# Two columns of the horizontal bias in one matmul for two of three thirds, a second copy of the queries, and one buffer for the rounded biases

## What is computed

```python
qkv = (x.reshape(B, S, dim) @ qkv_w + qkv_b).reshape(B, S, 3, nh, hd)
attn = jnp.einsum('bqc,bkc->bqk', q * scale, k)
rel_h = jnp.einsum('bhwc,hkc->bhwk', r_q, Rh)
rel_w = jnp.einsum('bhwc,wkc->bhwk', r_q, Rw)
attn = (attn.reshape(B * nh, h, w, h, w) + rel_h[:, :, :, :, None] + rel_w[:, :, :, None, :]).reshape(B * nh, S, S)
attn = jax.nn.softmax(attn, axis=-1)
out = (attn @ v).reshape(B, nh, h, w, hd)
return out @ proj_w + proj_b
```

## Times and profile before

| | |
|---|---|
| median of 3 runs | 6956.17 us (6955.4 to 11830.54) |
| profiled execution | 6956.88 us, its span 6955.1 us |
| mean granted TensorE clock | 0.988 |
| PE busy | 97% of the span |
| DVE, ACT, POOL busy | 79%, 68%, 13% |
| DMA engines busy | 65%, 146 GB/s on average |

### The profile page before, as it was taken

How to read it: one execution, slowest core, us unless ns; L and a number is a source line. 1 busy time by engine, 2 the same in 40 slices (tenths; PEclk the granted TensorE clock), 3 DMA queues, 4 the chain that set the end, 5 groups by cost and what they waited for, 6 DMA issues and landing times.

```text
span 6955.1 us, 139199 instructions
## 1 busy us (share of the span) xinstructions
PE 6778.3 (97%) x53600; PEld 4259.6 (61%) x53600; DVE 5488.7 (79%) x10165; ACT 4705.9 (68%) x10033; POOL 932.6 (13%) x967
## 2 busy tenths in 40 slices
PE   6999999999999999999999999999999999999998
PEld 4666666666666666666665666656666566666664
DVE  6887888778887788877888778887788878877883
ACT  2777676667666677666776767667676676766775
POOL 2112010110102110121111111102101121101110
PEclk8999999999999999999999999999999999999999
DMA  5667676666767667676666666766667666666663
GB/s 141 143 147 159 135 151 144 157 155 136 152 133 161 148 140 155 141 164 139 148 142 147 156 144 142 154 144 157 143 141 155 137 162 141 141 149 143 147 146 90
DMA packets 306306, 1013.72 MB, mean 146 GB/s; under 512 B 107440, under 2 KB 196976, under 8 KB 215920
## 3 DMA queue, kind: packets, MB, share of 16 engines
q1 hardware_dynamic: 305648, 1004.81, 64.9%
HBM read 745.26 MB, written 255.69 MB: 144 GB/s over the span
## 4 chain that ended last, share of the span: by engine, by line
PE 92%; DMA 3%; DVE 2%; ACT 2%; issue 0%; POOL 0%; SPq 0%; POOLq 0%; DVEq 0%; ACTq 0%
PE work L791 28%; PE work L861 26%; PE work L782 25%; PE work L807 6%; DMA moving<-rel_scratch 3%; PE work L826 2%; PE work L845 2%; ACT probs L547 2%; PE work L834 1%; DVE mpart L660 1%; PE work L813 0%; DMA qk_scratch<-back 0%; DVE xb L651 0%; POOL back L495 0%; DVE stats L610 0%
## 5 line engine op out<-in xcount | busy, mean ns | idle before, releaser
L660 DVE TENSOR_REDUCE mpart<-work 128x1 f32<-128x512 f32 (+1 forms) x8640 | 5094.3, 631 | 1164.7 <-PE work L791 1101.2
L547 ACT ACTIVATE probs<-work 128x512 f32<-128x512 f32 (+1 forms) x8640 | 4086.2, 565 | 977.9 <-PE work L782 962.8
L791 PE MATMUL work<-mkeys,hi 128*128 128x512 f32 (+1 forms) x8640 | 3424.1, 398 | 28.9 <-ACT probs L547 13.9
L782 PE MATMUL work<-moving,keys 113*128 113x512 f32 (+1 forms) x8640 | 3309.2, 384 | 76.7 <-DMA moving<-rel_scratch 71.8
L791 PEld LDWEIGHTS work<-mkeys,hi 128*128 128x128 f32 x8640 | 1653.0, 191 | 668.3 <-DVE mpart L660 369.0
L861 PE MATMUL work<-probs,vall 128*17 128x288 f32 x27648 | 2019.0, 410 | 0.0
L782 PEld LDWEIGHTS work<-moving,keys 113*128 113x128 f32 x8640 | 1652.1, 191 | 414.3 <-DMA moving<-rel_scratch 75.0
L861 PEld LDWEIGHTS work<-probs,vall 128*17 128x17 f32 x27648 | 637.9, 97 | 861.3 <-ACT probs L547 361.1
L480 POOL TENSOR_TENSOR full<-full,hi 128x384 f32<-128x384 f32 x576 | 579.5, 1006 | 1382.5 <-DVE hi L705 1382.5
L807 PEld LDWEIGHTS work<-image,tab 128*48 128x48 f32 x6912 | 401.9, 124 | 544.3 <-ACT probs L547 478.6
L535 ACT ACTIVATE full<-work 48x384 f32<-48x384 f32 x576 | 278.5, 483 | 527.9 <-PE work L807 527.9
(11 more groups left out here) (42 smaller groups left out, 650.2 us busy)
## 6 DMA issues: line engine op xcount, KB each, us to landing
moving<-rel_scratch SPq DMA_DIRECT2D x1728, 144.0 KB
moving<-qk_scratch SPq DMA_DIRECT2D x288, 576.0 KB
rel_scratch<-hi SPq DMA_DIRECT2D x192, 432.0 KB, 5.9
rel_scratch<-full SPq DMA_DIRECT2D x192, 432.0 KB, 5.4
moving<-rel_scratch SPq DMA_DIRECT2D x288, 288.0 KB
image<-qk_scratch SPq DMA_DIRECT2D x384, 144.0 KB, 4.2
keys<-qk_scratch SPq DMA_DIRECT2D x192, 288.0 KB, 4.8
qk_scratch<-split_hi SPq DMA_DIRECT2D x144, 192.0 KB, 3.9
```

Source lines behind the costliest of these rows:

```text
L547: act.activation(probs[:, tile % RING, lo:up], bank[:, 0:up - lo], ACT.Exp).then_inc(act_read, 1)
L660: dve.tensor_reduce(mpart[:, u % 2, q, m:m + 1], bank[:, 0:MSPLIT[m][1] - MSPLIT[m][0]], AX.X, ALU.max)\
L782: pe.matmul(bank[:, 0:up - lo], tile_of(keys[0:K_ROWS, u % 2, :], c, third), moving[0:K_ROWS, slot_of(u, third)[0], lo:up], start=True, st ...
L791: pe.matmul(bank[:, 0:up - lo], hi[:, u % 2, q * P:(q + 1) * P], mkeys[:, u % 2, lo:up], start=True, stop=True).then_inc(for_dve, 1)
```

## The change

- The horizontal items r = 6 to 9 now cover the columns w and w + 16 (the first two thirds) together: four matmuls of 96 moving columns (2 runs of 48 that stand 16 elements apart) instead of eight of 48. The items 10 and 11, the last third, stay as they are. ACT copies the new form with another access pattern and the same number of elements.
- For this the queries of the first two thirds are kept a second time, in `image2`, so that the two columns meet their own weights: column w in partitions 0 to 63 and column w + 16 in 64 to 127, zeros elsewhere. `image_load` issues a DMA of 96 KB into it after each of its four. `tab` has a third table, the horizontal one with its lower half shifted by 16.
- `hi` is one buffer instead of two. `high` therefore waits for the last maximum of the unit before that reads the block, and its six places move from (8..13, 2) to `HIGH_AT`. The store of `hi` moves from tile 13 to 14 and that of `full` from 14 to 15, behind that tile's `top_load`.

```diff
+HIGH_AT = [(10, 2), (10, 4), (11, 2), (11, 4), (12, 2), (13, 5)]
-        hi = sb("hi", [P, 2, N], F32R)
+        hi = sb("hi", [P, N], F32R)
+        image2 = sb("image2", [P, 2 * SIDE * WIDE], F32R)
-        tab = sb("tab", [P, LAYERS, 2, TBW], F32R)
+        tab = sb("tab", [P, LAYERS, 3, TBW], F32R)
+        def column_third(p, x):
+            return image2[64 * p:64 * p + 64, x * SIDE * WIDE:(x + 1) * SIDE * WIDE]
...
                     for part in range(2):
                         sp.dma_start(row_half(x, x)[part::2].bitcast(F32), src).then_inc(image_in, 16)
+                        sp.dma_start(column_third(x, x)[part::2].bitcast(F32),
+                                     q_rows(u)[:, x * SIDE * WIDE:(x + 1) * SIDE * WIDE]).then_inc(image_in, 16)
...
-                    if t == 13 and u + 2 < UNITS:
-                        sp.wait_ge(hi_ready, NB * (u + 3))
-                        rel_store(u + 2, hi[:, (u + 2) % 2, :].bitcast(F32), 0, rel_hi_stored)
                     if t == 14 and 0 <= u + 1 < UNITS:
                         top_load(u + 1, 0)
                     if t == 14 and u + 2 < UNITS:
-                        sp.wait_ge(lo_ready, NB * (u + 3))
-                        rel_store(u + 2, full[:, :], 1, rel_lo_stored)
+                        sp.wait_ge(hi_ready, NB * (u + 3))
+                        rel_store(u + 2, hi[:, :].bitcast(F32), 0, rel_hi_stored)
...
                     if t == 15 and 0 <= u + 1 < UNITS:
                         top_load(u + 1, 1)
+                    if t == 15 and u + 2 < UNITS:
+                        sp.wait_ge(lo_ready, NB * (u + 3))
+                        rel_store(u + 2, full[:, :], 1, rel_lo_stored)
...
-                    to = to[:, (r - 6) // 2, :, 8 * (r % 2):8 * (r % 2) + 8]
+                    if r < 10:
+                        to = to[:, 0:2, :, 4 * (r - 6):4 * (r - 6) + 4]
+                        got = bank[0:SIDE, 0:BLK].rearrange("p (s w h) -> p s h w", s=2, w=4)
...
-                dve.wait_ge(act_read, place["rel", u, 7 + r // 2 * 2] + 1)
+                dve.wait_ge(act_read, place["rel", u, 9 if r < 4 else 11] + 1)
...
-                    if u >= 2:
-                        dve.wait_ge(rel_hi_stored, 32 * (u - 1))
+                    if u:
+                        dve.wait_ge(rel_hi_stored, 32 * u)
+                if u:
+                    dve.wait_ge(dve_read, place["max", u - 1, 3 * r + 2, MAXB - 1] + 1)
...
-                    for i in range(4 if r < 6 else 8):
+                    for i in range(4 if r < 10 else 8):
+                        elif r < 10:
+                            d, at, query = 2, 4 * (r - 6) + i, columns[:, :, :, 4 * (r - 6) + i]
+                            to = bank[0:SIDE, 0:BLK].rearrange("p (s i h) -> p s i h", s=2, i=4)[:, :, i, :]
```

More of the change, by code:

```diff
@@ L479, in low @@
                 pool.wait_ge(hi_ready, NB * u + r + 1)
-                pool.tensor_tensor(full[:, cols], full[:, cols], hi[:, u % 2, cols].bitcast(F32), ALU.subtract)\
+                pool.tensor_tensor(full[:, cols], full[:, cols], hi[:, cols].bitcast(F32), ALU.subtract)\
                     .then_inc(lo_ready, 1)
@@ L533, in rel_out @@
                     to = full[64:64 + SIDE, :].rearrange("p (s h w) -> p s h w", s=THIRDS, w=WIDE)
-                    to = to[:, (r - 6) // 2, :, 8 * (r % 2):8 * (r % 2) + 8]
-                    act.activation(to, bank[0:SIDE, 0:BLK].rearrange("p (w h) -> p h w", w=8), ACT.Copy)\
-                       .then_inc(act_read, 1)
+                    if r < 10:
+                        to = to[:, 0:2, :, 4 * (r - 6):4 * (r - 6) + 4]
+                        got = bank[0:SIDE, 0:BLK].rearrange("p (s w h) -> p s h w", s=2, w=4)
+                    else:
+                        to = to[:, 2, :, 8 * (r % 2):8 * (r % 2) + 8]
+                        got = bank[0:SIDE, 0:BLK].rearrange("p (w h) -> p h w", w=8)
+                    act.activation(to, got, ACT.Copy).then_inc(act_read, 1)
             def consume(item):
@@ L736, in _ @@
                             invert(u - 1)
-                        if 8 <= t < 14 and i == 2 and -2 <= u and u + 2 < UNITS:
-                            high(u + 2, t - 8)
                         if (t, i) == (TILES - KEEP - 1, 5) and 0 <= u + 1 < UNITS and u >= -1:
                             top(u + 1)
+                        if -2 <= u and u + 2 < UNITS and (t, i) in HIGH_AT:
+                            high(u + 2, HIGH_AT.index((t, i)))
                         if s + 1 < STAGES and j == 3:
@@ L754, in _ @@
             pe.wait_ge(const_set, 6)
-            pe.wait_ge(pool_set, 3)
+            pe.wait_ge(pool_set, 5)
             grid = image[:, :].rearrange("p (s h w) -> p s h w", s=THIRDS, w=WIDE)
             pairs = image[:, :].rearrange("p (x h w) -> p x h w", x=NB, w=WIDE)
+            columns = image2[:, :].rearrange("p (s h w) -> p s h w", s=2, w=WIDE)
             def ready_for_scores(tile, i):
@@ L790, in fill @@
                         pe.wait_ge(mkeys_in[u % 2], 32 * (u // 2 + 1))
-                    pe.matmul(bank[:, 0:up - lo], hi[:, u % 2, q * P:(q + 1) * P], mkeys[:, u % 2, lo:up],
+                    pe.matmul(bank[:, 0:up - lo], hi[:, q * P:(q + 1) * P], mkeys[:, u % 2, lo:up],
                               start=True, stop=True).then_inc(for_dve, 1)
@@ L892 @@
     halves = lambda w: w.reshape(LAYERS, 2, HALF, w.shape[-1]).transpose(0, 2, 1, 3)
-    rel = np.zeros((P, LAYERS, 2, TBW), np.float32)
+    rel = np.zeros((P, LAYERS, 3, TBW), np.float32)
     for layer, (p, _, _, _) in enumerate(names):
@@ L901 @@
             rel[64:128, layer, d, shift:2 * SIDE - 1] = table[:, 0:2 * SIDE - 1 - shift]
+        rel[0:64, layer, 2] = rel[0:64, layer, 1]
+        rel[64:128, layer, 2, WIDE:2 * SIDE - 1] = table[:, 0:2 * SIDE - 1 - WIDE]
     key = np.arange(N)
```

17 lines of the change are left out of this document (9 added, 8 removed).

## The result

The changed kernel takes 6970.49 us (median of 17 executions, 6964.1 to 6973.93) against 6960.14 us for the kernel before in the same comparison. The ratio is 1.0015, with a 95% interval from 1.0008 to 1.0022: about 10 us more where I had forecast 57 us less. One of the 17 executions of the kernel before lasted 11830.54 us; nothing shows why, and the median hardly feels it. The profiled execution has a span of 6967.4 us (mean granted clock 0.989) against 6955.1 us.

The account below looks back on a forecast made before the run. PE, busy 97% of the span, was taken as the bound. -69 (items) + 0 (DVE) + 4 (loads) + 3 (stores) + 4.5 (start) = -57.5 us against 6956.9 us, so 6900 us, range 6882 to 6985.

Parts of the forecast that it names:

- The items, -69 us: Tiles 6 to 9 on PE: 16 fewer matmuls a unit at 0.045 us each, 69 us less over 96 units.
- the per-element one: Tiles 6 to 9: spread columns cost 0.33 ns extra per element, cutting the gain to 27 us.
- a bound at two cycles a column: Tiles 6 to 9: 96 spread columns take 80 ns, an item 0.32 us, leaving a gain of 15 us.
- the second rival: Tiles 6 to 9: strided columns cost per element, gain 15 to 27 us, total about 6947 us; chance 0.17.
- The store of `full`, +3 us: Stores one tile later: `full` still lands 1.2 us before ACT's first bias copy; 3 us added for units running late.
- the third rival: Unit start: `full` lands too late, ACT and PE wait in about 60 units, 6989 to 7061 us; chance 0.20.
- What is late next: Behind the store of `full`: `slot_load` of tile 16, done by 1773.1, needed at tile 2, some 7 us after 1770.
- The loads of the columns, +4 us: Tile 12: four more DMAs of 96 KB hold SP 2.5 us; the bias row for tile 16 still arrives in time.
- The bound of 54: Upper end for the extra loads: 16 x 3.4 us, if the whole load falls on the path each time.
- DVE, 0: Tiles 10 to 12: two roundings make DVE at most 0.1 us late, covered by PE; cost 0, uncovered 10 us.
- The start, +4.5 us: Start of the run: first query loads 2.5 us later, DVE's table steps under 2 us longer; 4.5 us more.
- Waits for bias rows: PE's waits for bias rows coming back by DMA: stay at 16, near 72 us.

Follow-up runs that it names:

- e2: Kernel before, with items 6 to 9 as four matmuls of 96 neighbouring columns (wrong products), buffers, stores and loads unchanged: 6896.6 us, ratio 0.9914.
- e3: Kernel before, with one `hi` buffer, the new rounding places, DVE's wait and stores at tiles 14 and 15; old matmul forms, no `image2`: 6989.92 us, ratio 1.0043.
- e9: Kernel before, with only the store of `full` moved to tile 15, behind that tile's `top_load`: 6958.66 us, ratio 1.0.
- e10: Kernel before, with only the store of `hi` moved to tile 14, directly ahead of the store of `full`: 6964.55 us, ratio 1.0006.
- e8: Changed kernel, with column steps of 1, 2, 4 and 8 for items 6 to 9 and 48 neighbouring columns for item 10: one run, 6958.08 us.
- e1: Kernel before, with items 6 to 9 as four matmuls of 96 columns 16 apart, read from `image` (products partly wrong): 6932.47 us, ratio 0.9961.

## Why the prediction was wrong, point by point

- **The items, -69 us: mis-sized, -29.5 us.** The count of matmuls and the price of 0.045 us each nearly held (e2: 63.7 us in all tiles). The step that failed is "I take the full gain: an extra that is nearly equal at both clocks looks like a start-up". It is no start-up: it is a rate of 0.87 ns a column that hardly knows the clock. I had both readings of the earlier trace rows before me. I had put the per-element one at 0.33 ns and a bound at two cycles a column, which no row gave; the runs lie near that bound, 84 ns instead of 80, and the tile at 3.69 us, as the second rival had said ("if they last 3.69 or more, the second rival holds"). The argument I set against the bound, that 48 and 96 columns would last alike at 1.2 GHz, took the length of a record for its pace: in the trace of before, the 48 spread columns and the 96 in runs both start 80 ns apart there.
- **The store of `full`, +3 us: mis-sized, +30 us (e3).** This is the third rival, at the far less dramatic size of a stall in one unit in five. Two steps failed. "starts at 1759.78 and lands 5.8 us later, at 1765.6" counts from the first of two DMAs; the second was issued at 1760.9 and landed at 1766.7, so the cover was 3.4 us and not 4.5, and 0.1 us after the move, not 1.2. (The sum of both issues, 1.55 us in the earlier trace rows, already says that they do not leave together.) And "with equal landing time the cost is 0", with 0.3 us for crowding on the transfer's side: the crowding shows in the issue, where SP needs 2.54 us instead of 0.9. In e9 0.8 us of cover are left, and the time is that of before. The stall that I computed for 60 units all alike lengthened tile 0 in 19 units; 18 of these are among the 46 in which ACT starts as soon as the store has landed.
- **What is late next.** I had named the `slot_load` as next behind the store, needed 7 us later, and stopped. Behind it stands the `top_load` of tile 16, needed with it at the start of tile 2, and the waits for it account for the 13.8 us of tile 1: 27 waits of the weight loads, 14.6 us, where the kernel before has none. The need was put at the right place, and what stood behind the load was left out.
- **The loads of the columns, +4 us: mis-sized, 15 us** (the intervals of the two ratios allow 7 to 22). The bound of 54 held. I had looked at the bias row of tile 16 only: it is late 3 times, 2.0 us together. Of the 9 us that the traces place, 3.2 stand in tiles 0 to 2, behind the stores, and 5.2 in tiles 13 to 15; by which transfer each comes is not shown.
- **DVE, 0: right in the sum, by luck.** The net is +2 us in tiles 11 to 13 in e3 and +4 in the kernel after. But the step "DVE is never more than 0.1 us late" was read in a unit where DVE has no extra work. In the fourth head of seven stages PE waits 0.65 us and 0.96 us for DVE, and tiles 11 and 12 grow by 7.7 us each over these units; it shows so little because the same units wait for a late bias row behind it, and tile 13 gives 12.1 us of it back. Without those late rows the term would have been some 15 us, by my estimate from these lengths.
- **The start, +4.5 us: right**, 4.2 us.
- **Waits for bias rows: right** in size (62.2 us against 71.8), though there are 20 instead of 16; the difference of 9.6 us is less than the 12.1 us by which the tiles 13 behind the new DVE waits are shorter.
- **The sum** with the measured terms is -29.5 + 32.2 (tiles 0 to 2) + 4.3 (tiles 11 to 13) + 1.6 (the other tiles) + 4.2 (start) = +12.8 us, against 12.3 by the spans. Each rival was given as if it came alone: the second (6947 us) and a small form of the third came together. That the result lies within the range of 6882 to 6985 us is luck: the range reached that far for a stall in 60 units, and the time moved the other way than forecast.

## What to carry to other kernels

A saving in instruction count must be priced with the access pattern that the new instructions have: a form that hides beneath the weight load's pace says nothing of what twice as many columns cost. When a transfer is moved later, count its landing from the last DMA's issue, write down every transfer behind it in the queue up to the first one that is needed soon, and judge a cover by its small end over all units and not by its median: e9 and e10 leave 0.8 and 0.7 us in the median, but in 14 of 93 units e10 leaves none. Look at the units with the most extra work, not only at a quiet one. Two edits that cost 0 and 6 us alone (a later store, a nearer neighbour) stood together in a kernel that lost 30.

## What the runs showed of the hardware

- TensorE's moving float32r columns at steps of 2, 4, 8 and 16 elements start 83 to 91 ns apart for 96 columns with weight loads of 48, against 45 ns for neighbouring ones (e8, e1, kernel after, 2.4 GHz); the price is there from step 2 and does not grow. At 1.2 GHz it is 83 to 86 ns against 80 (kernel after).
- With a weight load of 48 columns of its own, a matmul starts 45 ns after the one before at 2.4 GHz whether it moves 48 neighbouring, 48 spread or 96 neighbouring columns (e8, e2).
- SP's issue of a DMA is not a constant: in unit 22 an issue of half of `full` took 0.41 to 0.45 us with the other store 8 us ahead (e9), 0.9 to 1.6 us with a store of 885 KB issued 3 us before (kernel after), and 2.1 to 2.2 us directly behind it (e10), while the time from issue to landing grew far less (at most 6.1, 6.0 and 7.0 us).
